# Four scheduling edits in a decoder kernel's rounding stage and its mixture-of-experts start-up

## The reference, cut to what matters

```python
def _div_clamp_fp8(x, scale):
    y = jnp.clip(x.astype(jnp.float32) / scale, -FP8_MAX, FP8_MAX)
    y = y.astype(jnp.bfloat16).astype(jnp.float32)
    return _fp8_roundtrip(y)
```

```python
logits = SOFTCAP * jnp.tanh((x @ w_gate) / SOFTCAP)
probs = jax.nn.softmax(logits, axis=-1)
_, idx = jax.lax.top_k(probs, TOPK)
mask = jax.nn.one_hot(idx, E, dtype=probs.dtype).sum(-2)
weights = probs * mask
for e in range(E):
    h = jax.nn.silu(x @ w1[e]) * (x @ w3[e])
    out = out + h @ w2[e] * weights[:, e:e + 1]
```

## Time and profile before

| | |
|---|---|
| median of three runs | 1427.23 us |
| lowest, highest | 1423.76, 1427.83 us |
| the profiled execution's own time | 1423.34 us |
| its span, first to last instruction | 1421.6 us |
| PE busy | 1319.8 us, 93% |
| DVE busy | 1077.4 us, 76% |
| ACT busy | 944.5 us, 66% |
| POOL busy | 904.3 us, 64% |
| rounding stage | about 345 to 376 us of the span |
| gate layer | about 1157 to 1167 us |
| experts' start-up | about 1167.7 to 1212 us |
| experts' loop, its last add landed | about 1401.8 us |

### The profile page before, as it was taken

How to read it: one execution, slowest core, us unless ns; L and a number is a source line. 1 busy time by engine, 2 the same in 40 slices (tenths; PEclk the granted TensorE clock), 3 DMA queues, 4 the chain that set the end, 5 groups by cost and what they waited for, 6 DMA issues and landing times. The chain is left out here.

```text
span 1421.6 us, 28335 instructions
## 1 busy us (share of the span) xinstructions
PE 1319.8 (93%) x8469; PEld 1096.3 (77%) x8469; DVE 1077.4 (76%) x2576; ACT 944.5 (66%) x3180; POOL 904.3 (64%) x1093
## 2 busy tenths in 40 slices
PE   9998888895799999999999999999999977999992
PEld 4445566663499999999999999899998855889881
DVE  5898758896788888888998888888888847444443
ACT  3997547775578887888887777777777846332331
POOL 4996237774177687786887766766767832455542
PEclk9999889998999999999999999999999999999996
DMA  9321110000101002002020020010100258576764
GB/s 342 154 119 59 36 46 2 2 2 1 60 2 63 28 1 98 2 31 71 23 79 33 1 90 2 24 67 2 46 1 27 71 174 300 134 170 159 165 160 133
DMA packets 55160, 105.83 MB, mean 74 GB/s; under 512 B 5053, under 2 KB 33669, under 8 KB 52709
## 3 DMA queue, kind: packets, MB, share of 16 engines
q1 hardware_dynamic: 46100, 84.90, 17.4%
q0 software_dynamic: 7488, 10.23, 4.5%
q10 hardware_dynamic: 1424, 8.91, 1.5%
HBM read 75.58 MB, written 28.44 MB: 73 GB/s over the span
## 5 line engine op out<-in xcount | busy, mean ns | idle before, releaser
L1852 ACT ACTIVATE pr_<-ps,neg_ 128x128 f32<-128x128 f32 x512 | 181.3, 366 | 64.9 <-DVE neg_ L1987 64.9
L1869 ACT ACTIVATE y<-ps,invsm 128x128 bf16<-128x128 f32 x512 | 146.4, 369 | 61.5 <-PE ps L1767 61.3
L1922 POOL TENSOR_TENSOR rstd<-var,half 128x6 f32<-128x6 f32 x128 | 172.5, 1347 | 10.1 <-POOL var L1917 0.2
L1933 POOL TENSOR_TENSOR z<-t,m 128x512 fp32r<-128x512 f32 x128 | 148.9, 1163 | 3.3 <-DVE t L2013 3.3
L1917 POOL TENSOR_TENSOR var<-stat,deps 128x6 f32<-128x6 f32 x128 | 26.2, 205 | 182.6 <-DVE stat L1967 182.5
L1749 PEld LDWEIGHTS ps<-qkt 128*128 128x128 f32 x1024 | 134.0, 191 | 10.4 <-ACT qkt L1836 2.8
L1778 PE MATMUL ps<-phi,z 128*128 128x256 f32 x512 | 138.2, 303 | 1.2 <-POOL z L1933 1.2
L1749 PE MATMUL ps<-qkt 128*128 128x128 f32 x1024 | 135.3, 275 | 2.5 <-ACT qkt L1844 2.4
L1926 POOL TENSOR_TENSOR pr_<-pr_,rec_ 128x512 f32<-128x512 f32 x128 | 133.6, 1043 | 1.4 <-DVE rec_ L1994 1.4
L1767 PE MATMUL ps<-XT 128*128 128x256 f32 x512 | 131.8, 380 | 2.8 <-ACT XT L1860 2.8
L1778 PE MATMUL ps<-plo,z 128*128 128x256 f32 x512 | 127.2, 279 | 0.0
(11 more groups left out here) (352 smaller groups left out, 4035.0 us busy)
## 6 DMA issues: line engine op xcount, KB each, us to landing
f_w_low<-w_low SPq DMA_DIRECT2D x39, 512.0 KB, 3.7
centred<-raw_weights ACTq DMA_DIRECT2D x8, 1024.0 KB, 3.9
w_low<-w_dram SPq DMA_DIRECT2D x8, 1024.0 KB, 10.6
aw_st<-centred SPq DMA_DIRECT2D x7, 1024.0 KB, 6.0
raw_weights<-wself_dram SPq DMA_DIRECT2D x4, 1024.0 KB, 13.8
raw_weights<-wcross_dram SPq DMA_DIRECT2D x4, 1024.0 KB, 15.1
w_rest<-w_dram SPq DMA_DIRECT2D x8, 512.0 KB, 3.9
w_high<-w_top SPq DMA_DIRECT2D x8, 512.0 KB, 2.7
```

Of the source, the lines that this page charges most:

```text
L1852: ins = act.activation(pr[:, u.par, h, :], bS[:, h * S:(h + 1) * S], ACT.Exp, bias=neg[:, u.par, h:h + 1], accum_out=tot[:, u.par, h:h + 1])
L1869: ins = act.activation(y[:, u.par, h * S:(h + 1) * S], bO[:, h * S:(h + 1) * S], ACT.Copy, scale=invsm[:, head:head + 1])
L1922: pool.tensor_tensor(rstd[:, u.par, 0:6], v, half[:, :], ALU.pow).then_inc(s_rstd, 1)
L1933: pool.tensor_tensor(z[:, u.par, :], t[:, u.par, :], m[:, u.par, :], ALU.subtract).then_inc(s_z, 1)
```

## The change

Five things are edited.

1. Rounding: column 0 is scaled by ACT in two halves, and DVE does clamp, power and magic on the first half and then on the second, in place of each pass over both halves. PE starts with three matmuls on the identity, before its first wait.
2. Gate: SP issues the gate's load and the four pieces ahead of the two stores.
3. Who makes the rests: PE and ACT pieces 0, 3, 7; POOL pieces 1, 2, 4, 5 (new, same instruction, after POOL's constants and ahead of its wait for the row numbers); DVE piece 6. ACT's order becomes split 1, keep 0, split 2, 3, 4, keep 3, split 5, 6, 7, keep 7. PE's subtract(2) and keep(2) are gone.
4. PE's wait for all lows moves from ahead of the loop to the first up, so that the first two turn_x stand before it.
5. SP's two loads of w2's high part move from behind pieces 4 to 7 to behind waits for the owners, the row numbers and the first tile's gathered rows (d_x[0]), ahead of the ring.

```diff
-WARM_UNITS, WARM_PRODUCTS, WARM_AT_END, BY_PE = 4, (3, 4), 15, (0, 2, 3, 7)
+WARM_UNITS, WARM_PRODUCTS, WARM_AT_END = 4, (3, 4), 15
+BY_PE, BY_POOL, BY_DVE = (0, 3, 7), (1, 2, 4, 5), (6,)
...
         def _(pe):
+            for _ in range(3):
+                pe.matmul(ps[7][:, 0:2 * P], ident[:, :], ident[:, :].unsqueeze(1).to_broadcast([P, 2, P]), start=True, stop=True)
             pe.wait_ge(s_signs, 4)
...
-                act.activation(y[:, n % 3, :], XT[:, n % CB, :], ACT.Copy,
-                               scale=quant.inv[:, n // CB, n % CB:n % CB + 1]).then_inc(s_y, 1)
+                for h in (halves if n == 0 else [slice(0, TOK)]):
+                    act.activation(y[:, n % 3, h], XT[:, n % CB, h], ACT.Copy,
+                                   scale=quant.inv[:, n // CB, n % CB:n % CB + 1]).then_inc(s_y, 1)
...
+            def round_up(n):
+                if n == 0:
+                    for i in range(2):
+                        clamp(n, i)
+                        power(n, i)
+                        magic(n, i)
+                    return
+                for step in (clamp, power, magic):
+                    for i in range(2):
+                        step(n, i)
...
-    def split_low(self, dve, q):
+    def split_low(self, eng, q):
         i, e = self.place(q)
-        dve.wait_ge(self.s_hi, q + 1)
-        dve.tensor_tensor(self.low[:, i, e, :], self.low[:, i, e, :].bitcast(F32),
+        eng.wait_ge(self.s_hi, q + 1)
+        eng.tensor_tensor(self.low[:, i, e, :], self.low[:, i, e, :].bitcast(F32),
                           self.high[:, i, e, :].bitcast(F32), ALU.subtract).then_inc(self.s_lo, 1)
...
             def _(sp):
+                sp.dma_start(gate[:, :, 0:E], io["w_gate"].rearrange("(k p) n -> p k n", p=P)).then_inc(d_gate, 16)
+                experts.load_up(sp, io, range(0, UP_PIECES // 2))
                 for name in ("rows_x", "sums"):
                     sp.dma_start(io[name][(B - 1) * S:B * S, :], X[:, B - 1, :]).then_inc(experts.stored, 16)
-                sp.dma_start(gate[:, :, 0:E], io["w_gate"].rearrange("(k p) n -> p k n", p=P)).then_inc(d_gate, 16)
-                experts.load_up(sp, io, range(0, UP_PIECES // 2))
...
                 experts.load_up(sp, io, range(UP_PIECES // 2, UP_PIECES))
-                experts.load_w2(sp, io)
                 sp.wait_ge(experts.stored, experts.STORES)
                 sp.wait_ge(s_own, 1)
                 sp.wait_ge(s_ids, 2)
+                sp.wait_ge(d_x[0], 16)
+                experts.load_w2(sp, io)
...
-                subtract(2)
                 subtract(3)
...
                 pe.wait_ge(s_own, 1)
-                pe.wait_ge(experts.s_lo, UP_PIECES - len(BY_PE))
-                pe.wait_ge(s_left, len(BY_PE) * PIECE * CB)
                 pe.wait_ge(s_ids, 2)
...
                 def up(u):
                     pe.wait_ge(s_xe, u.n + 1)
+                    if u.peeled and u.n == 0:
+                        pe.wait_ge(experts.s_lo, len(BY_POOL) + len(BY_DVE))
+                        pe.wait_ge(s_left, len(BY_PE) * PIECE * CB)
...
                 keep(0)
-                experts.split_high(act, 2)
-                experts.split_high(act, 3)
-                keep(2)
+                for q in range(2, 5):
+                    experts.split_high(act, q)
                 keep(3)
-                for q in range(4, UP_PIECES):
+                for q in range(5, UP_PIECES):
                     experts.split_high(act, q)
                 keep(7)
...
+                for q in BY_POOL:
+                    experts.split_low(pool, q)
                 pool.wait_ge(s_ids, 2)
...
-                experts.split_low(dve, 1)
                 dve.wait_ge(s_map, 2 * B // CHUNK)
...
-                experts.split_low(dve, 4)
-                experts.split_low(dve, 5)
-                experts.split_low(dve, 6)
+                for q in BY_DVE:
+                    experts.split_low(dve, q)
```

More of the change, by code:

```diff
@@ L1469, in round_codes @@
     HALF = TOK // 2
+    halves = [slice(h * HALF, (h + 1) * HALF) for h in range(2)]
     y = sbuf(ctx, "y0", [P, 3, TOK], BF16)
@@ L1528, in _, with clamp, power, magic @@
         def _(dve):
[L1529 to L1538, removed]
+            def clamp(n, i):
+                dve.wait_ge(s_y, n + 2 if n else i + 1)
+                h = halves[i]
+                dve.tensor_scalar(y[:, n % 3, h], y[:, n % 3, h], FP8_MAX, -FP8_MAX, ALU.min, ALU.max).then_inc(s_clamp, 1)
+            def power(n, i):
+                dve.wait_ge(s_clamp, 2 * n + i + 1)
+                h = halves[i]
+                dve.tensor_scalar(p2[:, n % 2, h].bitcast(U16), y[:, n % 3, h].bitcast(U16), 0x7F80, None,
+                                  ALU.bitwise_and).then_inc(s_power, 1)
+            def magic(n, i):
                 if n >= 2:
                     dve.wait_ge(s_z, (n - 1) * TILES)
[L1541 to L1544, removed]
+                dve.wait_ge(s_power, 2 * n + i + 1)
+                h = halves[i]
+                dve.tensor_scalar(m[:, n % 2, h], p2[:, n % 2, h], FP8_MIN_NORMAL, ROUND, ALU.max, ALU.mult
+                                  ).then_inc(s_magic, 1)
+            def round_up(n):
[8 more added lines that the diff above has]
+                        step(n, i)
             def copied(n):
```

## The result

The changed kernel takes 1445.8 us (median of four runs, 1445.5 to 1446.45) against 1426.82 us for the kernel before in the same runs: a ratio of 1.0138, 95% interval 1.0122 to 1.0154. It is slower by 19.0 us of median.

What follows compares the result with a forecast made beforehand. The prediction took the single line of waits up to the first down product as the bound. Its terms, -2.2 + 17.3 + 1.8 = +16.9 us, gave 1440.2 on the profile or 1444.1 on the median; forecast 1442, range 1431 to 1450.

Steps and rivals of the forecast that it cites:

- The exclusion: Routing chain: DVE instructions with two SBUF inputs stand until POOL's 4.5 us subtraction ends; mask +11.5 us, chunks +4.5.
- what PE loses at a lower clock in the counts, +0.2: PE's counts in the routing chain: +0.2 us for a lower clock, nearly cancelled by a wait of -0.25.
- the short wait that goes: Chunks: DVE's short wait for PE's chunk goes, -0.25 us, nearly cancelling +0.2 in the counts.
- Dropping subtract(2): PE and ACT ahead of the chunks: dropping subtract(2) and keep(2) gives nothing, since both now wait on the mask.
- w2 behind the first rows: First down product: w2's first low part lands 14.5 to 16.2 us after the rows; +17.3 us with everything upstream included.
- The stretch behind: Down product after PE's stand for w2: matmuls at lower clock cost +1.8 us, ends 0 and 2.4.
- One sign: Experts' layer, profile after: the first turn_x stands behind the gather, not behind DVE; forecast at 1214.5, 13.1 us later.
- Rounding: Rounding stage: DVE's column 2 starts earlier, -2.2 us, with -1.0 and -2.4 as ends.
- Gate: Gate layer: piece 0's load is issued 0.84 us earlier, ahead of the stores, so -0.84 us at the barrier.
- (a): Rival, routing chain: POOL and DVE do not exclude each other; 1423 to 1427 us, no change; chance 0.12.
- (b): Rival, first up and down product: as the no-exclusion case, and w2 does not gate; faster, 1418 us; chance 0.04.
- (c): Rival, routing chain: milder exclusion, one or two of four waits go, 4.5 to 9 us; 1432 to 1437; chance 0.14.

Runs made afterwards that it cites:

- the fill: Changed kernel with POOL filling the rests of pieces 1, 2, 4, 5 with zero in place of subtracting: 1428.89 us, ratio 1.0019.
- one piece: Kernel before with only DVE's first subtraction (piece 1) moved to POOL: 1431.53 us against 1426.63, ratio 1.0034.
- the edit alone: Kernel before with the third edit whole (rests of pieces 1, 2, 4, 5 on POOL) and no other: 1447.54 us against 1426.63.
- The filled run: Changed kernel with ten more matmuls on the identity between PE's first and second chunk: 1443.12 us, ratio 1.0114.

## Why the prediction was right, point by point

**Direction and size.** Forecast 1442 (1431 to 1450), measured 1445.8. The sum on the median of the runs, 1444.1, was 1.7 us off; the 1442 between it and the profile's level was a choice that moved away from the result. As a change the sum was +16.9 and the medians moved by +19.0.

**The exclusion** was the deciding step, taken from one meeting of two instructions in the trace before, and it held to a few tenths: POOL's instruction at 4.53 us (4.5 forecast from two shorter kinds), the mask 12.38 us later against the layer (12.3), the three held instructions the very ones named, one chunk instruction held for 4.3 (4.5). That it is this, and not the waits or the order, is shown by the fill (mask back at 6.9 us), by one piece (+4.9) and by the edit alone (+21).

**What failed: PE's clock in the chunks.** The prediction let "what PE loses at a lower clock in the counts, +0.2" stand against the short wait that goes. PE's four chunks were left at their old duration. Three of them ran at 1.2 GHz, 3.5 in place of 2.0 us; row numbers came 5.74 us behind DVE's last chunk, where 2.1 stood. That is +3.6, and nearly all of the 3.8 between the forecast and the measured weights' end. The filled run shows the price: with the full clock the 3.7 us are back. I had priced the lower clock at the down product and not asked the same of the chunks, though the change both lengthens PE's stand ahead of three of them and takes work away before them.

**Dropping subtract(2)** was put at nothing, and that may be the same mistake. In all five kernels without it and without the filling matmuls the last three chunks, or all four, ran at 1.2 GHz, with DVE on time too (the run in which POOL only writes). In all six kernels with it they ran at 2.4 GHz, with the mask 4.0 us late too (one piece on POOL). But no run keeps subtract(2) while three routing instructions are held, and the order of ACT's splits goes with it. So whether the stand of 4.75 us or the missing work cost the 3.6 us stays open.

**w2 behind the first rows.** The rows landed 3.0 us after their issue (4.0 forecast), w2's high part landed 15.1 us after them, and PE first used the low part 16.4 us after them, behind four matmuls at half clock; 14.5 to 16.2 was forecast for the low part. The stretch behind was 2.1 us longer (1.8 forecast); PE's rows are back at full clock at 1238.9, 6.5 us behind the stand. Taking the load back gave 4.1 us, not the whole stand of 4.9 and 2.1: the same wait had kept the ring off the second gather. One sign did not come: the first turn_x did not stand behind the gather but ran at 1217.98 straight behind PE's own late subtract(7), 1.0 us after the rows. It cost nothing, since w2 came later still.

**Rounding**: 2.14 for 2.2, 1.9 at the stage's end; by the other profiles 1.3 to 2.2. **Gate**: 1.66 for 0.84, and 1.5 to 2.9 by the other profiles, so this term was too small. Piece 0 was ready for ACT 6.4 us after the layer's first DMA, 8.1 before; the issue shift explains 0.93 of the 1.66. What explains the rest (two stores fewer ahead of it in the queue, perhaps) no run isolates. Gate and chunks are errors of opposite sign, 0.8 against 3.8, and make the total look somewhat better than its parts. The profiles differ by 23.1, not 19.0, because 2.7 us more lie in the first and third rows of the ledger.

**The rivals.** (a) and (b) needed the engines to pass each other; they do not. (c), a milder exclusion, did not occur: all four of POOL's instructions held one of DVE's for 4.0 to 4.3 us of their 4.5 to 4.8.

## What to carry to other kernels

Before work goes to POOL, look at what DVE does in those microseconds: if DVE's instructions read two SBUF tensors, or are small casts or tensor_scalars, one long POOL instruction can stop the whole chain for most or all of its length, however short DVE's instructions are, and the profile books the wait as DVE being busy. Such a move has a second price, PE's clock: ask it of every stand that grows and of every place where PE loses work. Of a change with several edits, price each alone: here the rounding edit, the gate edit and PE's moved wait bring 4.7 us together, 7.3 with the ring's loads held for the first rows, and the rests on POOL alone cost 21.

## What the runs showed of the hardware that I had not expected

- PE stayed at 1.2 GHz through 10 us in which it was busy all the time (PEclk 0.50, PE 10.00 of 10.00, the chunks' matmuls). The same 64 matmuls took 7.4 us at 2.4 GHz straight behind the subtractions of the kernel before. PE busy in the profile is no sign that its clock is at the full level.
- A DVE tensor_scalar of eight f32 columns stood 1.83 us for a POOL fill that reads nothing; a two-input instruction of 128 columns under such a fill did not.
- Under POOL instructions of 5.4 us with one input, DVE's two-input instructions came free 1.6 us before POOL's end, three times; a cast stood to the end. Why, no run shows.
- The twelve profiled executions (before, after and ten experiments) reached ACT's first scaling, with the same code ahead of it, between 344.9 and 348.5 us of their spans. That is 3.6 us of scatter ahead of every edit, and why stages have to be compared from their own start. How much of the scatter between runs (1422.2 to 1430.2 us for the kernel before) lies there is not shown.
